# A decoder layer on one core: the order of work in the prologue, and zeros for TensorE before the data comes

## The chip, the core and the metric

The kernel runs on one core of a Trainium2 chip. TensorE multiplies, ScalarE evaluates functions and evacuates results, VectorE and GpSimd do elementwise work, and SyncE issues the transfers from HBM. The engines run side by side, each through its own list of instructions in order; they wait for each other only at semaphores. The metric is the time of one execution on the device in microseconds (us), as the median of several runs.

## The reference

One decoder layer over 4 sequences of 256 tokens with 256 features, in f32, batch-wise independent:

```
x = x + attn(layernorm(x))     # 16 heads: q,k = layernorm(silu(causal conv4(h @ Wq|Wk)));
                               # v = h @ Wv; beta = sigmoid(h @ Wb + bb); gate = silu(h @ Wg)
                               # S_t = (1-b_t) S_(t-1) + b_t v_t k_t^T;  o_t = S_t q_t;  (o*gate) @ Wo
x = x + xattn(layernorm(x))    # query, key = ctx @ Wq.T + bq, ctx @ Wk.T + bk; softmax(query key^T)
x = x + moe(layernorm(x))      # 16 routed experts (4 chosen per token) + a shared one
```

What matters here: the first step of everything is a layer norm of x, while the query and key of the cross attention depend on the context input alone, and are not needed until the 16 heads are done.

## The kernel before

The 1024 tokens are eight tiles of 128, or two halves (`c` = 0, 1) of 512. Weights and activations of the projections are split into a high half, which is a copy rounded to `fp32r`, and a low half, the f32 value minus that copy; `mm3` (L1344 to L1348) makes one product as three: high by low, low by high, high by high. ScalarE makes the high copies of weights (`high`, L605), GpSimd the low halves (`split_low`, L437). Plain f32 products go through `mm` (L1341).

The program has a section for each engine, and in each the instructions are written in the order in which they run; loops are unrolled in pairs of heads. No scheduler changes it. The heads run as a software pipeline in steps. Ahead of that stands a prologue:

- SyncE issues the loads in the order x (two halves), the context's weights, the context, its biases, the identity, beta's weights, and then the weights of the first two heads.
- VectorE clears two tiles (`obetT`, L989, and `dmask`, L990), takes statistics of x (`x_stats`), works out the norm factors (`norm_factors`, signalled by `ln_rstd`), and normalises four of the eight tiles (`half_norm`, L977). ScalarE normalises the other four (L585). Then VectorE copies the identity into parts of `dmask` (L1004, L1005); the columns P to L of each of its four blocks stay zero.
- TensorE makes four context products (`context_qk`, L1362) and 16 transposes of the normalised tiles (`half_transpose`, L1350), three products ahead of the transposes and one behind. ScalarE evacuates the products (`context_out`, L597) and copies the transposed tiles out as `xT_hi` (`half_out`, L589); VectorE makes `xT_lo` (`half_low`, L981).
- `project_in(0, 0, 0)` is the first head's first projection. It needs `w_lo` of the first head and both halves of `xT`. From here on TensorE's list is dense: projections of q, then beta, then k and gate, and so on. ScalarE and VectorE take their results through the taps of the convolution (`first_taps`, L625; `taps`), GpSimd adds the last tap (`last_tap`, L453).
- `wv_hi` and `wv_lo` are the split value weights of the first pair of heads. ScalarE's functions come in tables; where the next function isn't in the loaded one, an `ACT_TABLE_LOAD` stands ahead of it (Sigmoid at L716, Silu at L652).

Of the kernel before, what the change touches and what calls it, by code (L numbers as in the profile page):

```python
# [22 lines left out]
ACT = mybir.ActivationFunctionType  # L23
AX = mybir.AxisListType

P = 128
B, L, D = 4, 256, 256
# [3 lines left out]
N = 512  # L31
# [16 lines left out]
ROUTED_SCALE = 2.5  # L48
EPS = 1e-5
RSQRT_SEED = 1597463007.0  # L50
VERY_NEGATIVE = -3.0e38
# [75 lines left out]
def decoder_layer(nc, x_in, ctx_in, xw_in, xb_in, wb_in, bb_in, w_in, prm_in, wv_in, wo_in,  # L127
# [5 lines left out]
    with ctx:  # L133
# [3 lines left out]
        def sem(name):  # L137
            return ctx.enter_context(nc.semaphore(name))
# [143 lines left out]
        b_lo_ready, r_lo_ready = sem("b_lo_ready"), sem("r_lo_ready")  # L282
        obet_ready, dmask_ready = sem("obet_ready"), sem("dmask_ready")
        r_full, r_score = sem("r_full"), sem("r_score")
        r_tok_full, r_tok_ready = sem("r_tok_full"), sem("r_tok_ready")
# [150 lines left out]
        def _(pool):  # L436
# [36 lines left out]

            pool.wait_ge(ln_rstd, NCH)
            split_low(0, 0)
            low_values(0, 0)
            split_low(0, 1)
            last_tap(0, 0, range(2 * NCH))

# [100 lines left out]
        def _(act):  # L580
# [16 lines left out]
            def context_out(u):  # L597
# [3 lines left out]
                                     bias=xb[:, u // NCH:u // NCH + 1]).then_inc(x_qk_ready, 1)  # L601

            act.wait_ge(ld["beta"], 32)
            nc.scalar.activation(wb_hi, wb, ACT.Copy).then_inc(small_split, 1)
            def high(g, k):  # L605

                s = k % 2
                w = slice(s * 3 * D, (s + 1) * 3 * D)
                act.wait_ge(ld_w[s], uses(g, k, 2) * 16)
                if not (isinstance(g, int) and G * g + k < 2):  # L610

                    act.wait_ge(a_full, units(g, k - 1, 6))
                nc.scalar.activation(w_hi[:, w], w_raw[:, w], ACT.Copy).then_inc(w_hi_ready, 1)
# [80 lines left out]
            def high_projection(pair, s):  # L694
# [3 lines left out]
                nc.scalar.activation(wo_hi[:, w], wo_raw[:, :], ACT.Copy).then_inc(wo_hi_ready, 1)  # L698

            high(0, 0)  # L700
            act.wait_ge(ld_wv[0], 16)
            nc.scalar.activation(wv_hi[:, 0:N], wv_raw[:, 0:N], ACT.Copy).then_inc(wv_hi_ready, 1)
            context_out(0)
            context_out(1)
            for c in range(NCH):
                half_norm(0, c)
            context_out(2)
            for c in range(NCH):
                half_out(0, c, xT_hi)
            context_out(3)  # L710
            high(0, 1)
            first_taps(0, 0, (0, 1))

            for c in range(NCH):
                act.wait_ge(b_full, c + 1)
                nc.scalar.activation(betaT[:, c * N:(c + 1) * N], bank[2 + c][0:H, :], ACT.Sigmoid,  # L716
                                     bias=bb).then_inc(b_ready, 1)
            first_taps(0, 0, (2, 3))
            gates(0, 0, range(NCH))
            first_taps(0, 1, (0, 1))  # L720
# [196 lines left out]
        def _(dve):  # L917
# [70 lines left out]

            obet_zero = steps.did(nc.vector.memset(obetT, 0.0))  # L989
            a = steps.did(nc.vector.memset(dmask[:, :], 0.0))  # L990

# [8 lines left out]
            dve.wait_ge(ld["const"], 16)  # L1000
            steps.after(a)
            dm = dmask[:, :].rearrange("p (b c) -> p b c", b=B)
# [105 lines left out]
            dve.wait_ge(b_ready, NCH)  # L1108
            steps.after(obet_zero)
            bt = betaT.rearrange("h (b t) -> h b t", b=B)  # L1110
# [229 lines left out]
        def _(pe):  # L1340
# [26 lines left out]

            context_qk(0)
            context_qk(1)
            pe.wait_ge(ld["const"], 16)  # L1370
            context_qk(2)
            for c in range(NCH):
                half_transpose(0, c)
            context_qk(3)

# [457 lines left out]
```

## Time and profile before

| | us |
|---|---|
| median of 3 runs | 578.58 (578.08 to 578.64) |
| the profiled execution | 578.73 |
| its span, first to last instruction | 576.9 |
| TensorE busy | 554.7 (96%) |
| VectorE, ScalarE, GpSimd busy | 432.5, 398.1, 292.7 |
| mean granted clock of TensorE | 0.997 |

The span is what the trace shows; the 1.8 us around it are start and end of the execution. A row of the timeline gives the start in us from the first instruction, the length, engine, line, operation and tiles (out<-in), how many instructions are merged in it, and in brackets the idle time of the engine just ahead and what ended it. Tiles that share memory have the name of the memory: `values` is also the normalised x, `raw` the context, `gate` also beta's weights, `gated_hi` also their high half. PE is TensorE, ACT ScalarE, DVE VectorE, POOL GpSimd, SPq SyncE's queue.

### The profile page before, as it was taken

The page shows a single profiled execution, that of the slowest core. Times are in us where ns is not written, and L with a number is a line of the kernel's source. Part 1 is how long each engine was busy: PE and PEld are TensorE (multiplying, and loading weights), DVE is VectorE, ACT ScalarE, POOL GpSimd, SP SyncE. Part 2 cuts the span into 40 slices and gives each one's busy share as a digit, 9 for nine tenths or more (in the row PEclk, how much of TensorE's full clock was granted, in tenths as well). Part 3 has the DMA queues.
Part 4 walks back from the last instruction along what each step waited for, and adds up shares of the span by engine and source line. Part 5 has one row for each costly group of instructions (what it writes and reads, how often), then busy time and mean ns, then how long its engine had stood idle before and what let it go on. Part 6 is the DMA issues. An engine that isn't in the chain of part 4 may idle for free.

```text
span 576.9 us, 9944 instructions
## 1 busy us (share of the span) xinstructions
PE 554.7 (96%) x3392; PEld 485.0 (84%) x3392; DVE 432.5 (75%) x1046; ACT 398.1 (69%) x782; POOL 292.7 (51%) x194
## 2 busy tenths in 40 slices
PE   4898999999999999999999999989899999999997
PEld 1597889989989999899899898878678888888887
DVE  8769989998998899889989998978956543323333
ACT  3979988979779789798797887786653334333431
POOL 2335756746666457366565673420021565556552
PEclk9999999999999999999999999999999999999999
DMA  6132032032030130230211202210020433233321
GB/s 201 31 120 84 0 120 84 1 119 83 3 120 25 59 120 2 82 107 15 84 51 70 83 1 102 82 30 2 1 56 5 164 129 98 95 129 127 94 81 73
DMA packets 18001, 42.31 MB, mean 73 GB/s; under 512 B 4736, under 2 KB 6528, under 8 KB 17952
## 3 DMA queue, kind: packets, MB, share of 16 engines
q1 hardware_dynamic: 17952, 41.69, 21.6%
q8 instruction: 27, 0.44, 0.3%
q14 instruction: 22, 0.18, 0.1%
HBM read 40.47 MB, written 1.21 MB: 72 GB/s over the span
## 4 chain that ended last, share of the span: by engine, by line
PE 85%; DVE 7%; ACT 4%; issue 1%; DMA 1%; SPq 1%; DVEq 0%; ACTq 0%
PE bank L1346 21%; PE bank L1348 20%; PE bank L1347 20%; PE bank L1342 14%; PE bank L1486 5%; PE bank L1474 4%; ACT tok L671 2%; DMA w_raw<-in_w 1%; DVE stats L1051 1%; DVE xT_lo L986 1%; DVE stats L971 1%; DVE x L1187 1%; ACT values L585 1%; DVE x L1336 0%; DVE raw L1070 0%
## 5 line engine op out<-in xcount | busy, mean ns | idle before, releaser
L1346 PE MATMUL bank<-xT_lo,w_hi 128*128 128x512 f32 x320 | 133.7, 418 | 1.9 <-DVE conv L1070 1.2
L1348 PE MATMUL bank<-xT_hi,w_hi 128*128 128x512 f32 x320 | 125.9, 394 | 0.0
L1347 PE MATMUL bank<-xT_hi,w_lo 128*128 128x512 f32 x320 | 125.3, 392 | 0.0
L464 POOL TENSOR_TENSOR gated_lo<-gated,gated_hi 128x512 fp32r<-128x512 f32 x30 | 38.8, 1293 | 116.5 <-ACT gated_hi L691 112.8
L671 ACT ACTIVATE tok<-bank,nmr,rstd 128x128 f32<-128x128 f32 x256 | 91.2, 503 | 2.0 <-DVE nmr L966 2.0
L1346 PEld LDWEIGHTS bank<-xT_lo,w_hi 128*128 128x128 f32 x320 | 60.5, 189 | 16.3 <-DVE conv L1070 3.2
L459 POOL TENSOR_TENSOR raw<-tap,raw 128x506 f32<-128x506 f32 x32 | 62.0, 1936 | 20.3 <-DVE raw L1070 16.3
L459 POOL TENSOR_TENSOR conv<-tap,conv 128x506 f32<-128x506 f32 x32 | 62.0, 1936 | 20.1 <-DVE conv L1070 20.1
L1348 PEld LDWEIGHTS bank<-xT_hi,w_hi 128*128 128x128 f32 x320 | 60.2, 188 | 13.6
L1347 PEld LDWEIGHTS bank<-xT_hi,w_lo 128*128 128x128 f32 x320 | 60.7, 190 | 9.1
L1051 DVE BATCH_NORM_STATS2 stats<-bank 128x6 f32<-128x128 f32 x256 | 56.4, 284 | 14.8 <-PE bank L1474 14.8
L1042 DVE TENSOR_TENSOR_SCAN decay<-obet,dmask 128x1536 f32<-128x1536 f32 x16 | 62.0, 3873 | 0.0
L1226 DVE TENSOR_TENSOR conv<-bank,tok 128x512 f32<-128x512 f32 x36 | 24.8, 690 | 44.2 <-PE bank L1348 44.0
L1234 DVE TENSOR_TENSOR gated_lo<-gate,gated_hi 128x512 fp32r<-128x512 f32 x32 | 24.0, 785 | 39.6 <-ACT gated_hi L849 39.6
L546 POOL TENSOR_TENSOR gate<-conv,tap 128x512 f32<-128x512 f32 x32 | 42.5, 1332 | 21.4 <-DVE conv L1226 13.2
L849 ACT ACTIVATE gated_hi<-gate 128x512 fp32r<-128x512 f32 x32 | 18.9, 628 | 48.0 <-PE bank L1348 41.0
L683 ACT ACTIVATE qk<-bank,prm 128x512 f32<-128x512 f32 x64 | 51.5, 844 | 0.0
L1070 DVE SCALAR_TENSOR_TENSOR raw<-bank,prm,raw 128x510 f32<-128x510 f32 x64 | 46.8, 743 | 5.6 <-ACT tap L639 4.5
L1342 PE MATMUL bank<-qk 128*128 128x256 f32 (+1 forms) x256 | 50.2, 329 | 0.5 <-DVE x L1103 0.3
L1070 DVE SCALAR_TENSOR_TENSOR conv<-bank,prm,conv 128x510 f32<-128x510 f32 x64 | 46.8, 743 | 3.4 <-ACT tap L639 2.3
L1342 PEld LDWEIGHTS bank<-qk 128*128 128x128 f32 x256 | 43.2, 190 | 5.7 <-issue 0.7
L1342 PE MATMUL bank<-probs,values 128*128 128x256 f32 (+1 forms) x256 | 47.0, 327 | 0.0
(184 smaller groups left out, 1398.4 us busy)
## 6 DMA issues: line engine op xcount, KB each, us to landing
obet<-obet_rows SPq DMA_DIRECT2D x16, 768.0 KB, 4.3
w_raw<-in_w SPq DMA_DIRECT2D x22, 384.0 KB, 4.8
tap<-route_rows SPq DMA_DIRECT2D x16, 512.0 KB, 4.0
w_raw<-in_w SPq DMA_DIRECT2D x12, 256.0 KB, 3.0
wv_raw<-in_wv SPq DMA_DIRECT2D x8, 256.0 KB, 4.8
wo_raw<-in_wo SPq DMA_DIRECT2D x8, 256.0 KB, 4.9
w_raw<-in_w SPq DMA_DIRECT2D x12, 128.0 KB, 2.1
x<-in_x SPq DMA_DIRECT2D x2, 512.0 KB, 4.7
```

What stands on the lines that cost most here:

```text
L459: nc.gpsimd.tensor_tensor(y, r, y, ALU.add).then_inc(conv_done, 1)
L464: nc.gpsimd.tensor_tensor(gated_lo[:, cc], gated[:, c * N:(c + 1) * N], gated_hi[:, cc].bitcast(F32), ALU.subtract).then_inc(gated_lo_read ...
L546: nc.gpsimd.tensor_tensor(weighted(m, c), prod[:, two(m, c)], wbc[:, s * T + c * N:s * T + (c + 1) * N], ALU.mult).then_inc(e_weighted, 1)
L671: ins = nc.scalar.activation(tok[:, t * P:(t + 1) * P], t_ring[u][:, i * P:(i + 1) * P], ACT.Identity, scale=rstd[:, t:t + 1], bias=nmr[:, ...
L683: nc.scalar.activation(qk[:, u * N:(u + 1) * N], t_ring[u][:, :], ACT.Identity, scale=prm[:, o:o + 1], bias=prm[:, o + 1:o + 2]).then_inc( ...
L1042: nc.vector.tensor_tensor_scan(decay[:, :], obet[:, :], dmask[:, :], 0.0, ALU.mult, ALU.add).then_inc(decay_ready, 1)
L1051: ins = nc.vector.bn_stats(stats[:, 6 * t:6 * t + 6], t_ring[u][:, i * P:(i + 1) * P])
L1070: ins = nc.vector.scalar_tensor_tensor(out=y, in0=r, scalar=prm[:, o + 3 - back:o + 4 - back], in1=y, op0=ALU.mult, op1=ALU.add)
L1342: return nc.tensor.matmul(o, l, r, start=start, stop=stop)
L1346: nc.tensor.matmul(o, l_hi, r_lo, start=start, stop=False, skip_group_check=loose)
L1347: nc.tensor.matmul(o, l_lo, r_hi, start=False, stop=False, skip_group_check=loose)
L1348: return nc.tensor.matmul(o, l_hi, r_hi, start=False, stop=stop, skip_group_check=loose)
```

## The change

Six things in the prologue; nothing behind it is touched.

1. TensorE multiplies zeros. VectorE clears `dmask` first and signals it by a new semaphore `zeros_ready`. TensorE waits for it, and makes `WARM` = 7 f32 products of 128 zeros by 256 columns of zeros from `dmask` into banks 0 and 1, which nobody reads before the transposes overwrite them.
2. All four context products stand in front of the transposes.
3. ScalarE evaluates a Sigmoid of one column of zeros as its first function.
4. ScalarE's list: layer norm first, then the first head's weights, the transposed activations and two of the context evacuations; the second head's weights go behind beta's Sigmoid, the value weights and the other two evacuations further back, among the gates.
5. GpSimd waits for VectorE's four norm tiles (`ln_norm_dve`) instead of the norm factors, and splits the second head's weights ahead of the first head's last taps; the value weights come between the taps.
6. VectorE's waits for its own clears go through `zeros_ready`.

```
 # GpSimd
-            pool.wait_ge(ln_rstd, NCH)
+            pool.wait_ge(ln_norm_dve, 2 * NCH)
             split_low(0, 0)
+            split_low(0, 1)
+            last_tap(0, 0, (0, 1))
             low_values(0, 0)
-            split_low(0, 1)
-            last_tap(0, 0, range(2 * NCH))
+            last_tap(0, 0, (2, 3))
 # ScalarE
+            act.wait_ge(zeros_ready, 1)
+            nc.scalar.activation(small[:, 0:1], dmask[:, P:P + 1], ACT.Sigmoid)
             act.wait_ge(ld["beta"], 32)
             nc.scalar.activation(wb_hi, wb, ACT.Copy).then_inc(small_split, 1)
...
+            for c in range(NCH):
+                half_norm(0, c)
             high(0, 0)
-            act.wait_ge(ld_wv[0], 16)
-            nc.scalar.activation(wv_hi[:, 0:N], wv_raw[:, 0:N], ACT.Copy).then_inc(wv_hi_ready, 1)
+            for c in range(NCH):
+                half_out(0, c, xT_hi)
             context_out(0)
             context_out(1)
-            for c in range(NCH):
-                half_norm(0, c)
-            context_out(2)
-            for c in range(NCH):
-                half_out(0, c, xT_hi)
-            context_out(3)
-            high(0, 1)
             first_taps(0, 0, (0, 1))
 
             for c in range(NCH):
...
+            high(0, 1)
             first_taps(0, 0, (2, 3))
-            gates(0, 0, range(NCH))
+            act.wait_ge(ld_wv[0], 16)
+            nc.scalar.activation(wv_hi[:, 0:N], wv_raw[:, 0:N], ACT.Copy).then_inc(wv_hi_ready, 1)
+            gates(0, 0, (0,))
+            context_out(2)
+            gates(0, 0, (1,))
+            context_out(3)
             first_taps(0, 1, (0, 1))
 # VectorE
-            obet_zero = steps.did(nc.vector.memset(obetT, 0.0))
-            a = steps.did(nc.vector.memset(dmask[:, :], 0.0))
+            nc.vector.memset(dmask[:, :], 0.0).then_inc(zeros_ready, 1)
+            nc.vector.memset(obetT, 0.0).then_inc(zeros_ready, 1)
...
-            steps.after(a)
+            dve.wait_ge(zeros_ready, 1)
 # TensorE
-            context_qk(0)
-            context_qk(1)
+            pe.wait_ge(zeros_ready, 1)
+            zeros = dmask[:, :].rearrange("p (b c) -> p b c", b=B)
+            for i in range(WARM):
+                mm(bank[i % 2][:, 0:L].rearrange("p (b c) -> p b c", b=2), zeros[:, 0, P:L], zeros[:, 2:4, P:L],
+                   True, True)
+            for u in range(2 * NCH):
+                context_qk(u)
             pe.wait_ge(ld["const"], 16)
-            context_qk(2)
             for c in range(NCH):
                 half_transpose(0, c)
-            context_qk(3)
```

How the lists stand on the two engines in front of the first projection, in the order in which they run. TensorE, from its first product to the first projection (`raw` holds the context, `values` the normalised x), before:

```order
L1342 MATMUL bank<-raw 128x512 [waits ld_ctx] x2
L1342 MATMUL bank<-raw 128x512 [waits ld_ctx,ld_const]
L1357 MATMUL bank<-ident,values 128x128 [waits ln_norm_dve,ln_norm_act]
L1357 MATMUL bank<-ident,values 128x128 x7
L1357 MATMUL bank<-ident,values 128x128 [waits ln_norm_dve,ln_norm_act]
L1357 MATMUL bank<-ident,values 128x128 x7
L1342 MATMUL bank<-raw 128x512 [waits ld_ctx]
L1346 MATMUL bank<-xT_lo,w_hi 128x512 [waits w_lo_ready,ln_split]
```

and now:

```order
L1350 MATMUL bank<-dmask 128x256 [waits zeros_ready]
L1350 MATMUL bank<-dmask 128x256 x6
L1350 MATMUL bank<-raw 128x512 [waits ld_ctx] x4
L1365 MATMUL bank<-ident,values 128x128 [waits ln_norm_dve,ln_norm_act,ld_const]
L1365 MATMUL bank<-ident,values 128x128 x7
L1365 MATMUL bank<-ident,values 128x128 [waits ln_norm_dve,ln_norm_act]
L1365 MATMUL bank<-ident,values 128x128 x7
L1354 MATMUL bank<-xT_lo,w_hi 128x512 [waits w_lo_ready,ln_split]
```

Seven products from `dmask` stand in front, the fourth context product has gone ahead of the transposes, and the first projection waits for the same two things as before.

ScalarE, from its first data to the taps of the first head (`attT<-bank` is a context evacuation, `values<-x` a norm tile, `xT_hi<-bank` a copy of transposed activations), before:

```order
L604 ACTIVATE gated_hi<-gate 128x32 [waits ld_beta]
L613 ACTIVATE w_hi<-w_raw 128x768 [waits ld_w0]
L702 ACTIVATE wv_hi<-wv_raw 128x512 [waits ld_wv0]
L600 ACTIVATE attT<-bank,xbias 128x512 [waits x_qk_full] x2
L585 ACTIVATE values<-x,nmr,rstd 128x256 [waits ln_rstd]
L585 ACTIVATE values<-x,nmr,rstd 128x256
L585 ACTIVATE values<-x,nmr,rstd 128x256 [waits ln_rstd]
L585 ACTIVATE values<-x,nmr,rstd 128x256
L600 ACTIVATE attT<-bank,xbias 128x512 [waits x_qk_full]
L593 ACTIVATE xT_hi<-bank 128x512 [waits ln_full] x4
L600 ACTIVATE attT<-bank,xbias 128x512 [waits x_qk_full]
L613 ACTIVATE w_hi<-w_raw 128x768 [waits ld_w1]
```

and now:

```order
L608 ACTIVATE small<-dmask 128x1 [waits zeros_ready]
L610 ACTIVATE gated_hi<-gate 128x32 [waits ld_beta]
L588 ACTIVATE values<-x,nmr,rstd 128x256 [waits ln_rstd]
L588 ACTIVATE values<-x,nmr,rstd 128x256
L588 ACTIVATE values<-x,nmr,rstd 128x256 [waits ln_rstd]
L588 ACTIVATE values<-x,nmr,rstd 128x256
L620 ACTIVATE w_hi<-w_raw 128x768 [waits ld_w0]
L596 ACTIVATE xT_hi<-bank 128x512 [waits ln_full] x4
L603 ACTIVATE attT<-bank,xbias 128x512 [waits x_qk_full] x2
L644 ACTIVATE conv<-bank,prm 128x512 [waits a_full,ld_prm0]
L646 ACTIVATE tap<-bank,prm 128x512
```

The norm tiles and the four copies have moved past the value weights and all context evacuations; two of the evacuations stand right behind the copies. The value weights, the other evacuations and the second head's weights are no longer in this stretch.

GpSimd, from its first split to the first head's last taps (`conv<-tap`), before:

```order
L444 TENSOR_TENSOR w_lo<-w_raw,w_hi 128x768 [waits w_hi_ready,ln_rstd]
L450 TENSOR_TENSOR wv_lo<-wv_raw,wv_hi 128x512 [waits wv_hi_ready]
L444 TENSOR_TENSOR w_lo<-w_raw,w_hi 128x768 [waits w_hi_ready]
L459 TENSOR_TENSOR conv<-tap,conv 128x2x253 [waits taps_done] x4
L459 TENSOR_TENSOR raw<-tap,raw 128x2x253 [waits taps_done]
```

and now:

```order
L446 TENSOR_TENSOR w_lo<-w_raw,w_hi 128x768 [waits w_hi_ready,ln_norm_dve]
L446 TENSOR_TENSOR w_lo<-w_raw,w_hi 128x768 [waits w_hi_ready]
L461 TENSOR_TENSOR conv<-tap,conv 128x2x253 [waits taps_done] x2
L452 TENSOR_TENSOR wv_lo<-wv_raw,wv_hi 128x512 [waits wv_hi_ready]
L461 TENSOR_TENSOR conv<-tap,conv 128x2x253 [waits taps_done] x2
L461 TENSOR_TENSOR raw<-tap,raw 128x2x253 [waits taps_done]
```

The first split waits for `ln_norm_dve`, and the second head's split has moved past the value split, which now stands between two pairs of taps.

## Rows read from the trace of the kernel before

**Rows 1.** The page, part 1: busy us, share, instructions.

```profile
PE 554.7 (96%) x3392; PEld 485.0 (84%) x3392; DVE 432.5 (75%) x1046; ACT 398.1 (69%) x782; POOL 292.7 (51%) x194
```

**Rows 2.** Chain of waits, 9 to 20 us and 47: start, length, what.

```profile
4.83 5.33 DMA w_raw<-in_w
...
10.18 0.84 ACT w_hi L613
11.03 0.52 ACT wv_hi L702
11.55 1.25 ACT attT L600 x2
12.80 1.97 ACT values L585 x4
14.76 0.57 ACT attT L600
15.34 0.49 ACT xT_hi L593
...
15.85 1.30 DVE xT_lo L986 x2
...
17.19 0.50 PE bank L1346
...
47.28 0.23 PE bank L1347
```

**Rows 3.** Timeline, TensorE: start, length, what, count.

```profile
8.29 5.38 PE L1342 MATMUL bank<-raw 128*128 128x512 f32 x6 [8.29 <-DMA xbias<-in_xb]
...
12.72 0.95 PE L1342 MATMUL bank<-raw 128*128 128x512 f32 x1
...
13.83 2.08 PE L1357 MATMUL bank<-ident,values 128*128 128x128 f32 x16 [0.16 <-ACT values L585]
15.74 1.02 PE L1342 MATMUL bank<-raw 128*128 128x512 f32 x2
...
16.18 0.59 PE L1342 MATMUL bank<-raw 128*128 128x512 f32 x1
...
30.41 0.40 PE L1346 MATMUL bank<-xT_lo,w_hi 128*128 128x512 f32 x1
```

**Rows 4.** Timeline, VectorE.

```profile
1.11 1.34 DVE L989 MEMSET gate<- 16x1536 f32 x1 [1.11 <-PEq L1825]
...
10.16 0.17 DVE L966 SCALAR_TENSOR_TENSOR nmr<-nw,rstd 128x8 f32<-128x8 f32 x1
...
11.34 1.90 DVE L977 TENSOR_SCALAR values<-x,rstd,nmr 128x256 f32<-128x256 f32 x1
...
13.16 1.30 DVE L1004 COPY dmask<-ident 128x128 f32<-128x128 f32 x1
...
33.53 2.97 DVE L1070 SCALAR_TENSOR_TENSOR raw<-bank,prm,raw 128x510 f32<-128x510 f32 x4 [4.47 <-ACT tap L639]
```

**Rows 5.** Timeline, GpSimd.

```profile
11.17 1.92 POOL L444 TENSOR_TENSOR w_lo<-w_raw,w_hi 128x768 fp32r<-128x768 f32 x1 [10.73 <-ACT w_hi L613]
13.05 1.33 POOL L450 TENSOR_TENSOR wv_lo<-wv_raw,wv_hi 128x512 fp32r<-128x512 f32 x1
...
35.14 1.28 POOL L459 TENSOR_TENSOR raw<-tap,raw 128x506 f32<-128x506 f32 x1 [4.93 <-DVE raw L1070]
```

**Rows 6.** Timeline, ScalarE.

```profile
21.64 1.28 ACT L716 ACT_TABLE_LOAD   x1
...
24.43 0.78 ACT L637 ACTIVATE conv<-bank,prm 128x512 f32<-128x512 f32 x1 [0.24 <-PE bank L1348]
...
34.61 2.19 ACT L659 ACTIVATE conv<-conv 128x512 f32<-128x512 f32 x4
```

**Rows 7.** Windows: PE, PEld, DVE, ACT, POOL busy, PEclk, DMA.

```profile
43.00:47.00 4.00, 1.77 (x14) 1.33 (x13) 3.89 (x8) 3.57 (x11) 2.74 (x3) 1.00 0.01 2
8.00:13.80 5.80, 5.38 (x6) 1.83 (x6) 5.38 (x19) 3.85 (x8) 2.63 (x2) 1.00 0.44 163
```

More of the change, by code:

```diff
@@ L49 @@
 EPS = 1e-5
+WARM = 7
 RSQRT_SEED = 1597463007.0
@@ L283, in decoder_layer @@
         obet_ready, dmask_ready = sem("obet_ready"), sem("dmask_ready")
+        zeros_ready = sem("zeros_ready")
         r_full, r_score = sem("r_full"), sem("r_score")
@@ L1108, in _ @@
             dve.wait_ge(b_ready, NCH)
-            steps.after(obet_zero)
+            dve.wait_ge(zeros_ready, 2)
             bt = betaT.rearrange("h (b t) -> h b t", b=B)
```

## The prediction

> **What bounds the kernel now.** I read the page first: TensorE is busy 554.7 us, 96% of the span [rows 1]. Nothing that the change touches lies behind the first head, so the question is how early TensorE's dense stream begins and whether everything behind it moves along. The second view is the chain of waits up to that beginning [rows 2]. It runs from the load of the first head's weights (lands at 10.16) through ScalarE alone: the split copy of those weights at 10.18 (0.84 us), the split of the value weights at 11.03 (0.52), two evacuations of context products at 11.55 (1.25), four layer norm tiles at 12.80 (1.97), a third evacuation at 14.76 (0.57), the first copy of the transposed activations at 15.34 (0.49). Then VectorE makes two low halves from 15.85 (1.30), and the first projection product starts at 17.19. The reader is to see that ScalarE is busy without a gap for 5.2 us there, and that 0.52 + 1.25 + 0.57 = 2.34 us of it are not needed by the product at 17.19.
>
> Third, TensorE's own timeline [rows 3]: it starts at 8.29, when the context has landed, with six passes of 512 columns (three of the four context products; an f32 product is two passes). The last starts at 12.72, so they come 0.89 us apart; the two passes of the fourth product, at 15.74 and 16.18, are 0.44 apart. The first six therefore ran at the 1.2 GHz level and the later two at 2.4 GHz, although the granted clock of the stretch 8.00 to 13.80 is given as 1.00 [rows 7]: here the pace tells the level, not the column. The 16 transposes from 13.83, in 2.08 us, are fast already. So the clock rose between 12.72 and 13.83, after 4.4 to 5.5 us of these passes.
>
> Fourth, VectorE and GpSimd [rows 4, 5]. The norm factors end at 10.16 + 0.17 = 10.33. Three of VectorE's four norm tiles fit between that and 11.34, 0.34 us each; the fourth takes 1.90 us from there, and the first copy into dmask 1.30 from 13.16, while GpSimd splits weights from 11.17 (1.92) and 13.05 (1.33): both end when a GpSimd instruction does.
>
> **The change part by part.**
>
> Zeros on TensorE. The first memset runs from 1.11 for 1.34 us [rows 4]; dmask's is now that one, so the zeros can start at about 2.5. Seven products of 256 columns are 14 passes of 0.89 / 2 = 0.44 us at the low level, 6.2 us: they end at 8.7 if the clock never rises meanwhile, and earlier if it does. 4.4 to 5.5 us after 2.5 is 6.9 to 8.0, so I take the clock as high when the context products start at about 8.5 (0.2 later than now, on their load). Four products are then 8 passes of 0.44, 3.5 us, to 12.0, with the fourth, which stood behind the transposes, in front.
>
> Norms first on ScalarE. They start at 10.37 instead of 12.80 and end at 10.37 + 1.97 = 12.34. VectorE's tiles, which GpSimd no longer disturbs since it now waits for them, end at about 11.34 + 0.34 = 11.7. The transposes start at about 12.0 (0.13 us each, 2.08 / 16), those of the second half at about 13.0, and the first bank, four of them, is full by 12.6. The weights' split copy follows the norms: 12.34 to 13.18. The copies of the transposed activations start there, at 13.2 instead of 15.34. From that copy to the product the chain takes 17.19 - 15.34 = 1.85 us: **15.05**. In other words the chain loses 2.34 us of other work and gains 0.19 in waiting for the norm factors (10.37 against 10.18), which is -2.15.
>
> GpSimd behind the norms. This puts a second operand on the path. The weights' high half is ready at 13.18 instead of 11.02, so the low half runs from 13.25 for 1.92 us [rows 5] and ends at 15.17: **15.2** with the step to TensorE. Before, it was done at 13.09 and hidden. It is now late by about the same as VectorE's half, and I take the later one: the first product starts at 15.2, **2.0 us earlier**. What is late next is GpSimd's split, then VectorE's.
>
> What that split collides with. The dmask copies lay between 13.16 and VectorE's next work at 15.85, blocked until GpSimd's end at 14.38; so their own time is at most 15.85 - 14.38 = 1.47 us, and from 11.7 they are over at 13.2, before it starts. VectorE's low halves run from 13.7 beside it. The nearest rows are GpSimd's add at 35.14, 1.28 us, beside VectorE's taps from 33.53, four in 2.97 us or 0.74 each [rows 4, 5]: VectorE reads PSUM there as in the low halves, and neither side stretches. I cost it at nothing; if they did exclude each other, VectorE would wait until 15.15, and the product would start 1.85 - 0.49 = 1.36 later, at 16.5. The Trainium skill, "SBUF — State Buffer", section "Who interferes with whom", says the same of the mechanism: the shared port pair is an exclusive lock, which VectorE's copies and scalar forms and its operations with two SBUF inputs take, and one with a single SBUF input doesn't. By that rule the two stretched rows at 11.34 and 13.16 are explained (the trace agrees, 1.90 against 0.34), and the low halves, with one input in PSUM, go free.
>
> Sigmoid's table first. Its load of 1.28 us at 21.64 [rows 6] goes; the first load, before any data has come, merely loads another table. It is worth nothing here: after it the next taps wait 0.24 us for TensorE at 24.43, so ScalarE had slack. Into that slack goes the split of the second head's weights (0.84), which stood ahead of the first taps. The second sigmoid waits for 24 products (12 of the projection, 12 of beta) at 0.23 [rows 2]: 15.2 + 5.5 + 0.4 = 21.1; with its own 0.6 and the split ScalarE is free at 22.5, against 24.43 - 2.0 = 22.4. GpSimd's split for the second head follows and ends at 24.4; TensorE needs it at 30.41 - 2.0 = 28.4 [rows 3]. GpSimd's value split now queues behind, with two taps ahead of it and two after it, until 24.4 + 4 x 1.28 + 1.33 = 30.9; ScalarE's Silu of the first head needs them at 34.61 - 2.0 = 32.6 [rows 6]. The value split copy and two context evacuations (0.52 + 2 x 0.6 us) fall into ScalarE's waits for TensorE ahead of 32; if they didn't, the second head's taps would be late by up to 0.5. On the queue the load of the third head's weights, which waits for the first split, leaves 2 us later than at present, and belongs to a head whose products come after 28.4; the loads behind it wait for beta, which comes earlier.
>
> Sum, against the profiled execution's 578.73 (span 576.9 and 1.8 around it; the median of the runs is 0.15 lower): -2.0 at the first product, 0 at every later step because each later wait of the prologue is on TensorE or on something that TensorE released. 578.6 - 2.0 = **576.6**. Ends: -2.15 if only ScalarE's chain counted, -1.4 if three passes of the context products were still slow (0.44 us more each, of which 0.6 is free, since the first bank is needed only at 13.2, and 0.15 by GpSimd's being later). The runs of before spread over 0.56 us, which is added to these.
>
> **The rivals.**
>
> *The zeros do not raise the clock.* Multiplying zeros may not be what raises it, or the moment may lie later than 4.4 to 5.5 us; no run here multiplies zeros. Then the context products start cold at 8.7; with the clock up 5.5 us later, at 14.2, six passes are slow, the transposes start at 15.0, the first bank is full at 15.5, and the product comes at 17.35: 578.7, no change. Against it: the six slow passes show that f32 passes do raise it. The trace has one rise, and cannot show the spread.
>
> *GpSimd and VectorE exclude each other after all.* Product at 16.5, gain 0.7: 577.9. The taps beside GpSimd's add speak against it [rows 4, 5].
>
> *A later step takes part of it back*, ScalarE's fuller list between 16 and 30 us or GpSimd's longer queue: each would show as a TensorE wait of 0.3 to 1 us: 577.2 to 577.9.
>
> *Slower: the clock falls before the first product.* The fourth context product no longer stands behind the transposes, so TensorE idles from about 13.9 to 15.2. If the clock went down there, the products would start at the 1.2 GHz level and stay on it for 4.4 to 5.5 us, as at the start; in that time half the work gets done, which costs 2.2 to 2.75 us, more than the 2.0 gained: 578.8 to 579.4. It decides once the first projection products come 0.46 apart instead of 0.23. Against it: between 43 and 47 us TensorE is busy 1.77 of 4.00 us, and the products right behind come 0.23 apart [rows 2, 7].
>
> **How the numbers follow.** Forecast 0.74 (its own range 576.0 to 577.1), no rise 0.09, exclusion 0.05, a later step 0.07, slower 0.05. The range 575.9 to 577.9 takes in the forecast, the exclusion and most of the later steps, and leaves out the no-change and the slower case. About 0.2%, 1.16 us, is what a measurement of this kernel can tell from no change, so faster means below 577.4: the forecast, half of the later steps and a share of the early ends of the other cases, 0.82; same 0.13; slower 0.05.
>
> **What would show it.** Right: zeros from about 2.5; context passes 0.44 apart, from 8.3 to 8.7 on; ScalarE's norms at 10.4; VectorE's fourth norm tile as short as its first; first product at 15.0 to 15.4, released by GpSimd's w_lo or VectorE's xT_lo; the gap to before still 1.8 to 2.1 us at 30 and at 50 us. Wrong: context passes 0.89 apart, or the first product at 16.4 or later, or a new TensorE wait before 50 us that brings the stream back to before's times.

## The result, and the profile after

The changed kernel takes 575.03 us (median of 9 runs, 574.92 to 576.86); the kernel before, run beside it, 578.53 (9 runs, 578.08 to 578.64). The ratio of the changed kernel's time to that of before is 0.9949, with a 95% interval of 0.9938 to 0.996 (further down in brackets): 3.5 us faster, where 2.0 was predicted, and below the predicted range. The profiled execution took 574.93 us, with a span of 573.1.

One thing about the numbers has to be said first. The times of either kernel don't scatter, they fall into groups whose medians lie 1.6 us apart. A run has none, one or two stretches of about 3.4 us in which the granted clock is 0.50, the 1.2 GHz level, and the mean granted clock of the run tells which: 0.999 or 1.000 with none, 0.996 or 0.997 with one, 0.993 or 0.994 with two. The fourteen traces show this for none and for one (a fall behind TensorE's last product is not counted); for the other runs the number of stretches is read from the mean clock, and no run with two was traced. In all runs of this study, counting the repeats of both kernels beside the experiments (the first nine runs of before are placed by their times):

| | no stretch: runs, median | one: runs, median | two |
|---|---|---|---|
| before | 25 of 86, 576.95 | 60 of 86, 578.50 | 1, 580.11 |
| changed | 12 of 30, 574.97 | 16 of 30, 576.56 | 2, 578.03 and 578.16 |
| difference | −1.98 | −1.94 | |

The prologue's rows first, in the order of the rows of before. The page, part 1 (busy us, share of the span, instructions), beside [rows 1]:

```profile
PE 554.8 (97%) x3406; PEld 487.2 (85%) x3406; DVE 428.9 (75%) x1046; ACT 396.9 (69%) x782; POOL 292.9 (51%) x194
```

TensorE's busy time is as before, with 14 instructions more, the zeros. The chain of waits (start, length, what), beside [rows 2]:

```profile
1.17 5.26 DMA x<-in_x
...
6.46 1.42 DVE stats L979 x4
...
10.39 2.07 ACT values L588 x4
12.46 0.75 ACT w_hi L620
...
13.35 1.82 POOL w_lo L446
...
15.31 0.47 PE bank L1354
```

The load of x, VectorE's statistics, ScalarE's four norm tiles, the weights' split copy, GpSimd's low half, the product. The value weights and the three context evacuations are gone from it, and the chain starts from x where it had started from w. TensorE (start, length, instruction, count, in brackets the idle time ahead and what ended it), beside [rows 3]:

```profile
2.52 4.89 PE L1350 MATMUL bank<-dmask 128*128 128x256 f32 x14 [2.52 <-DVE dmask L997]
8.33 3.70 PE L1350 MATMUL bank<-raw 128*128 128x512 f32 x8 [0.93 <-DMA xbias<-in_xb]
11.87 1.91 PE L1365 MATMUL bank<-ident,values 128*128 128x128 f32 x16
15.31 0.47 PE L1354 MATMUL bank<-xT_lo,w_hi 128*128 128x512 f32 x1 [1.53 <-POOL w_lo L446]
...
25.54 0.50 PE L1354 MATMUL bank<-xT_lo,w_hi 128*128 128x512 f32 x1 [1.19 <-DVE conv L1078]
...
28.47 0.39 PE L1354 MATMUL bank<-xT_lo,w_hi 128*128 128x512 f32 x1
```

The eight context passes take 3.70 us, 0.46 each, where the first six had taken 0.89. The first product comes at 15.31 instead of 17.19 and is released by GpSimd; the second head's product comes at 28.47 instead of 30.41. The timelines of the other three engines follow. VectorE of the changed kernel, beside [rows 4]:

```profile
10.39 1.38 DVE L985 TENSOR_SCALAR values<-x,rstd,nmr 128x256 f32<-128x256 f32 x4
...
13.71 2.48 DVE L994 TENSOR_TENSOR xT_lo<-bank,xT_hi 128x512 fp32r<-128x512 f32 x4 [0.85 <-ACT xT_hi L596]
```

GpSimd of the changed kernel, beside [rows 5]:

```profile
13.35 1.81 POOL L446 TENSOR_TENSOR w_lo<-w_raw,w_hi 128x768 fp32r<-128x768 f32 x1 [12.91 <-ACT w_hi L620]
22.57 1.93 POOL L446 TENSOR_TENSOR w_lo<-w_raw,w_hi 128x768 fp32r<-128x768 f32 x1 [7.41 <-ACT w_hi L620]
```

ScalarE of the changed kernel, beside [rows 6]:

```profile
10.39 2.07 ACT L588 ACTIVATE values<-x,nmr,rstd 128x256 f32<-128x256 f32 x4 [1.33 <-DVE nmr L974]
...
13.10 2.02 ACT L596 ACTIVATE xT_hi<-bank 128x512 fp32r<-128x512 f32 x4
...
22.50 0.78 ACT L644 ACTIVATE conv<-bank,prm 128x512 f32<-128x512 f32 x1
```

VectorE's four norm tiles take 1.38 us together; the one that ran beside GpSimd before had taken 1.90 alone. VectorE's four low halves take 2.48 us beside GpSimd's split, as they did before with GpSimd idle:

```profile
15.85 2.48 DVE L986 TENSOR_TENSOR xT_lo<-bank,xT_hi 128x512 fp32r<-128x512 f32 x4 [0.43 <-ACT xT_hi L593]
```

GpSimd's 1.81 is no longer than its 1.92 before: the two did not exclude each other.

So far this is about the predicted 2.0 us: these two traces lie 1.88 us apart at the first product, 1.94 at the second head's, and still 1.97 at four transposes some 15 us later (43.02 against 44.99). Most of the rest lies 400 us later, where the change does nothing. Here are the windows of before (start and end, length, busy time and count of each engine; the last three columns are the granted clock, DMA's share and GB/s):

```profile
414.00:415.50 1.50, 0.03 (x1) 0.00 (x0) 1.17 (x2) 1.50 (x4) 0.00 (x0) 1.00 0.00 0
...
416.50:419.50 3.00, 3.00 (x8) 1.93 (x7) 2.62 (x17) 0.98 (x1) 0.00 (x0) 0.50 0.00 0
```

TensorE's timeline of before in these windows:

```profile
415.67 0.41 PE L1346 MATMUL bank<-xT_lo,wv_hi 128*16 128x512 f32 x1 [1.65 <-DVE xT_lo L986]
...
416.54 0.63 PE L1346 MATMUL bank<-xT_lo,wv_hi 128*16 128x512 f32 x1
416.97 0.63 PE L1347 MATMUL bank<-xT_hi,wv_lo 128*16 128x512 f32 x1
```

The windows of the same place in the changed kernel:

```profile
411.84:413.34 1.50, 0.03 (x1) 0.00 (x0) 1.17 (x2) 1.50 (x4) 0.00 (x0) 1.00 0.00 0
...
414.00:417.50 3.50, 3.50 (x17) 2.58 (x16) 3.09 (x18) 2.15 (x4) 0.00 (x0) 1.00 0.00 0
```

TensorE's timeline of the changed kernel there:

```profile
413.51 0.40 PE L1354 MATMUL bank<-xT_lo,wv_hi 128*16 128x512 f32 x1 [1.64 <-DVE xT_lo L994]
...
414.22 0.40 PE L1354 MATMUL bank<-xT_lo,wv_hi 128*16 128x512 f32 x1
414.45 0.39 PE L1355 MATMUL bank<-xT_hi,wv_lo 128*16 128x512 f32 x1
```

The stall is the same (1.65 and 1.64 us, for VectorE's low half of the second group of tokens). Behind it the products of before come 0.43 us apart at a granted clock of 0.50, until about 419.6; those of the changed kernel come 0.23 apart at 1.00. The changed kernel is 2.16 us ahead where the stall ends (413.51 against 415.67) and 3.8 at the end of the span (573.1 against 576.9): the stretch is the 1.6 us between, and no instruction there differs.

### The profile page after: what moved, and what is told of

It reads as the page before. It is cut to its first block, busy times and chain, and to the rows that moved or that the text cites. A ratio compares the mean times of both kernels' runs of the same rounds, so it can differ in the third digit from the quotient of the medians.

```text
span 573.1 us, 9971 instructions
## 1 busy us (share of the span) xinstructions
PE 554.8 (97%) x3406; PEld 487.2 (85%) x3406; DVE 428.9 (75%) x1046; ACT 396.9 (69%) x782; POOL 292.9 (51%) x194
## 4 chain that ended last, share of the span: by engine, by line
PE 85%; DVE 8%; ACT 4%; issue 1%; DMA 1%; POOL 0%; SPq 0%; DVEq 0%; ACTq 0%; POOLq 0%
PE bank L1354 21%; PE bank L1356 20%; PE bank L1355 20%; PE bank L1350 14%; PE bank L1498 5%; PE bank L1486 4%; ACT tok L678 2%; DMA x<-in_x 1%; DVE stats L979 1%; DVE stats L1059 1%; ACT values L588 1%; DVE x L1195 1%; DVE x L1344 0%; DVE raw L1078 0%; DVE xT_lo L994 0%
```

## The experiments

The first theory (S in the quoted expectations) was that the 3.5 us are two things: 2.0 in the prologue, as predicted, and 1.6 from the stretch at 416, which the profiled run of before has and that of the changed kernel has not; its rival (D), that the lists of ScalarE and GpSimd later in the prologue give the rest. When the first experiments had shown groups of times, two theories stood against each other: M, that each run has a stretch behind a TensorE stall or none, and that the kernel sets how often; and C, that the share of such runs belongs to the chip or the hour and is the same for both kernels. In experiments 9 and 10, A and B are two answers on one term of the prediction.

**1. The new order without zeros.** The changed kernel with

```diff
-WARM = 7
+WARM = 0
```

> The changed kernel without its seven products of zeros. Both theories: the context passes run at the 1.2 GHz level again, six of them 0.89 us apart from 8.3, so the transposes start at about 14.5 instead of 11.9 and the first projection product comes at 16.9 to 17.1 (changed 15.31, before 17.19). Theory S, that the rest of the gain is the slow stretch of TensorE at 416 us in the kernel before, which comes or stays away with the same stall of TensorE ahead of it: 578.2 to 578.4 where it comes, 576.5 to 576.7 where it doesn't; if the time at which the stall comes decides it, most runs stay at 578.3. Rival D, that the rest of the gain comes from the new order of ScalarE's and GpSimd's lists later in the prologue: about 577.0 in all runs.

Measured: 577.11 (12 runs), ratio 0.999 [0.9979, 1.0001]; without a stretch 576.93 (7 runs), as before; with one 577.66 (5 runs, 577.53 to 577.97), 0.8 below before's. Neither theory had named the times with one. TensorE's timeline:

```profile
8.48 6.06 PE L1350 MATMUL bank<-raw 128*128 128x512 f32 x8 [8.48 <-DMA xbias<-in_xb]
14.37 1.91 PE L1365 MATMUL bank<-ident,values 128*128 128x128 f32 x16
16.98 0.50 PE L1354 MATMUL bank<-xT_lo,w_hi 128*128 128x512 f32 x1 [0.70 <-DVE xT_lo L994]
```

The eight context passes take 6.06 us instead of 3.70, hold up the transposes until 14.37, and the product comes 0.2 us earlier than before. The traced run is one of three at 576.43 to 576.54; the other four without a stretch are at 576.93 to 577.18. Without a risen clock the order is worth nothing in these four and 0.4 to 0.5 us in the three. Where the other five runs have their stretch, and why it costs them less, was not traced.

**2. The zeros without the order.** On the kernel before, with `WARM` = 7 (VectorE's two later waits for its clears go through `zeros_ready` too):

```diff
-            obet_zero = steps.did(nc.vector.memset(obetT, 0.0))
-            a = steps.did(nc.vector.memset(dmask[:, :], 0.0))
+            nc.vector.memset(dmask[:, :], 0.0).then_inc(zeros_ready, 1)
+            nc.vector.memset(obetT, 0.0).then_inc(zeros_ready, 1)
...
+            pe.wait_ge(zeros_ready, 1)
+            zeros = dmask[:, :].rearrange("p (b c) -> p b c", b=B)
+            for i in range(WARM):
+                mm(bank[i % 2][:, 0:L].rearrange("p (b c) -> p b c", b=2), zeros[:, 0, P:L], zeros[:, 2:4, P:L],
+                   True, True)
             context_qk(0)
```

> The kernel before with the seven products of zeros in front (and dmask cleared first), every other list as before. Both theories: the first projection product stays at 17.1 to 17.2, since ScalarE's list sets it. Theory S: if the moment at which TensorE's early work raises the clock decides the slow stretch at 416 us, 576.8 in most runs; if the time of the stall decides it, 578.5. Rival D: 578.5 in all runs.

Measured: 577.50 (11 runs), ratio 0.999 [0.9979, 1.0]; without a stretch 576.34 and 576.38, 0.6 below before's median, from two runs only; the other 9 of 11 runs have a stretch, with a median of 577.54, 1.0 below before's. Windows of the profiled run, and then TensorE's timeline of it:

```profile
11.20:13.50 2.30, 0.00 (x1) 0.00 (x0) 2.30 (x2) 2.30 (x6) 2.30 (x2) 1.00 0.00 0
...
15.00:18.00 3.00, 3.00 (x10) 1.81 (x9) 2.81 (x8) 2.15 (x6) 0.00 (x0) 0.50 0.12 39
```

```profile
2.52 6.05 PE L1344 MATMUL bank<-dmask 128*128 128x256 f32 x14 [2.52 <-DVE dmask L991]
8.40 2.80 PE L1344 MATMUL bank<-raw 128*128 128x512 f32 x6
13.51 2.55 PE L1359 MATMUL bank<-ident,values 128*128 128x128 f32 x16 [2.31 <-ACT values L587]
...
16.87 1.32 PE L1348 MATMUL bank<-xT_lo,w_hi 128*128 128x512 f32 x1
```

The context passes end early, TensorE stands for 2.31 us until ScalarE's norms, and some 1.4 us after it has begun again the clock goes to 0.50; the first product takes 1.32 us. This is what the prediction's slower rival feared, the lower level at the first product, though the stall is another: ahead of the transposes and not behind them. This run is 1.1 us longer than the two without. The product comes earlier than the expected 17.1 to 17.2, but not for the zeros alone: here the weights landed at 9.95 (10.16 in the trace of before), and in experiment 3's trace, whose prologue is that of before and whose weights also land at 9.95, the product comes at 16.89. How the zeros gain the 0.6 us is not shown.

**3, 4. Filling the stall at 414.** Three products of zeros into a free bank, on the kernel before and on the changed one:

```diff
             half_transpose(2, 0)
+            z = dmask[:, :].rearrange("p (b c) -> p b c", b=B)
+            for i in range(FILL):      # 3
+                mm(bank[2][:, 0:L].rearrange("p (b c) -> p b c", b=2), z[:, 0, P:L], z[:, 2:4, P:L], True, True)
```

> The kernel before with three products of zeros (f32, 256 columns, 1.3 us at full clock) on TensorE in the stall of 1.65 us at 414 us, ahead of the router's products. Theory S: the clock does not fall at 416, the products there come 0.23 apart, and the time is 576.8 (578.5 less 3.4 us at half rate, 1.7) in all runs. Rival D: 578.5, or a little more if the zeros delay the router.

> The changed kernel with the same three products of zeros in the stall. Theory S: every run at 574.9 to 575.1, none near 576.5. Rival D: the two groups of times of the changed kernel remain, two thirds at 575.0 and one third at 576.4 to 576.9.

Measured: before with the fill 578.27 (12 runs), ratio 0.9996 [0.9985, 1.0008]: none 5 runs (576.99), one 6, two 1. The changed kernel with it 575.04 (6 runs), ratio 0.9949 [0.9936, 0.9962]: none 5, one 1. The first theory's 576.8 in every run failed. The windows of the first one's profiled run, about another stall, that of 1.19 us ahead of 27.19 (TensorE waits for VectorE's taps):

```profile
26.00:27.10 1.10, 0.00 (x0) 0.00 (x0) 1.06 (x3) 1.08 (x3) 0.00 (x0) 1.00 0.66 89
...
28.50:31.50 3.00, 3.00 (x8) 2.26 (x7) 0.27 (x2) 0.60 (x1) 1.26 (x1) 0.50 0.85 272
```

This run had no stretch at 416, and one at 28.3. So it isn't one place: several stalls can have one behind them.

**5, 11. The changed kernel, unedited, again.**

> The changed kernel once more, for the shares of its two groups of times. Theory M (mixture): a run has one stretch of 3.4 us at the 1.2 GHz level behind a TensorE stall, or none; the group without it moved from 576.9 to 575.0 (the prologue, -1.95), the group with it from 578.5 to 576.6, and the share of runs with it fell from 27 of 38 to 4 of 15. Two groups again, 575.0 and 576.4 to 576.9, the upper one with a quarter to a half of the runs. Rival C, that the two groups belong to the chip or the hour and not to the kernel: the share of the upper group is that of the kernel before in this same call.

> The changed kernel a third time, to count. Theory M: 575.0 at clock 0.999 to 1.0, 576.4 to 576.9 at 0.996 to 0.997, 578.1 at 0.994; of the 21 runs so far 9, 10 and 2. If the change itself made the slow stretch rarer than in the kernel before (18 of 61 without), well over half of these runs come at 575.0; if the first nine runs of it were luck, about 4 in 10.

Measured: 576.51 (12 runs), ratio 0.9976 [0.9963, 0.999], with 3 runs without a stretch, 7 with one, 2 with two; and 576.53 (9 runs), ratio 0.9961 [0.9948, 0.9974], with 3, 6 and none. The same program is at 575.0 in one session and at 576.5 in the next two. In these two, the share of runs with a stretch (9 of 12, then 6 of 9) is that of before beside it (16 of 23, then 18 of 25), as theory C had it. The first repeat's profiled run has its stretch at a third place, in its windows and then in TensorE's timeline:

```profile
41.00:45.00 4.00, 1.78 (x14) 1.34 (x13) 3.88 (x8) 3.56 (x11) 2.73 (x3) 1.00 0.01 2
45.00:45.50 0.50, 0.50 (x4) 0.41 (x3) 0.50 (x2) 0.50 (x3) 0.50 (x1) 0.90 0.00 0
45.50:48.50 3.00, 3.00 (x11) 2.43 (x10) 3.00 (x1) 3.00 (x8) 3.00 (x2) 0.50 0.00 0
```

```profile
43.00 0.66 PE L1498 MATMUL bank<-ident,tok 128*128 128x128 f32 x4 [1.48 <-ACT tok L678]
44.40 0.66 PE L1498 MATMUL bank<-ident,tok 128*128 128x128 f32 x4 [0.74 <-ACT tok L678]
...
45.73 0.63 PE L1354 MATMUL bank<-xT_lo,w_hi 128*128 128x512 f32 x1
```

TensorE stalls for 1.48 and 0.74 us, with four transposes between; the granted clock is 1.00 until 45, 0.90 on average over the next half microsecond, and 0.50 from there.

**6, 7. Filling more stalls.** The kernel before with the fill at 414 and two products of zeros behind beta's transposes, in the stall ahead of 27; the changed kernel with the same two, and with two of the four context products put behind the transposes again, in the stall ahead of the first projection:

```diff
             beta_tokens()
+            fill(3, FILL_EARLY)        # 2
...
             half_transpose(2, 0)
+            fill(2, FILL)              # 3
```

```diff
-            for u in range(2 * NCH):
+            for u in range(HEAD_CTX):  # 2
                 context_qk(u)
...
+            for u in range(HEAD_CTX, 2 * NCH):
+                context_qk(u)
```

> The kernel before with zeros on TensorE in two of its stalls: two products behind beta's transposes (stall of 1.2 us at 26 us) and three behind the transposes at 414 us. Theory M: nearly all runs at 576.9 to 577.0, the upper group at 578.5 gone or below 2 in 10. Rival C: half or more of the runs still at 578.5. If the fills were only in the way: all runs later by up to 0.3.

> The changed kernel with the same two fills, and with the third and fourth context products behind the transposes, where TensorE stalls 1.5 us ahead of the first projection product. Theory M: all runs at 575.0, none at 576.4 or above. Rival C: the two groups of the changed kernel, at the share of the call.

Measured: 577.59 (12 runs), ratio 0.9996 [0.9985, 1.0008], 6 without and 6 with one, where theory M had expected fewer than 2 in 10 with one; its profiled run has it at 46.0 to 49.4, behind the stall that no zeros fill. And 574.99 (6 runs), ratio 0.9958 [0.9943, 0.9973], 5 without and 1 with one, which theory M had not expected at all. The fills cost nothing (576.89 and 574.95 without a stretch).

**8, 12. The weights' split first.** A version that the profile pointed to: ScalarE stands idle until 10.39 in the changed kernel, and the weights land at about 10, so their split copy can go ahead of the norms, and GpSimd's split comes off the end of the path. As experiment 7, with three context products in front and

```diff
+            high(0, 0)
             for c in range(NCH):
                 half_norm(0, c)
-            high(0, 0)
```

and VectorE's copies into dmask behind its low halves.

> As the one before, but with the first head's weights split on ScalarE ahead of its norm tiles (they land at 10.2, the norm factors come at 10.4), the dmask copies on VectorE behind its low halves, and only the fourth context product behind the transposes. GpSimd's split then runs from 11.8 to 13.6 and no longer ends last; ScalarE's first copy of the transposed activations starts at 12.95 instead of 13.10, and the first projection product comes 1.9 later, at 14.85 (changed 15.31): 574.5 to 574.6 in all runs. If GpSimd's split was not what ended last in the changed kernel, 575.0.

> The weights-first version with both fills and the fourth context product behind the transposes, a second time: 574.2 to 574.5 at clock 0.999 to 1.0, 575.7 to 576.1 at 0.996; the upper group in about 1 of 6 if the fills keep the clock up at three of its four stalls, in half or more if the single run of it in six was luck.

Measured: 574.37 (6 runs), ratio 0.9948 [0.9932, 0.9964], and 574.48 (6 runs), ratio 0.9943 [0.9925, 0.9961]; 9 of 12 runs without a stretch, median 574.36 (574.5 to 574.6 in all runs was expected). GpSimd's timeline of the first, and then TensorE's:

```profile
11.81 1.83 POOL L448 TENSOR_TENSOR w_lo<-w_raw,w_hi 128x768 fp32r<-128x768 f32 x1 [11.37 <-DVE values L987]
```

```profile
14.58 0.50 PE L1356 MATMUL bank<-xT_lo,w_hi 128*128 128x512 f32 x1
```

GpSimd is done at 13.64, and the product comes at 14.58, 0.7 us earlier than in the changed kernel and 0.3 earlier than expected; the end comes 0.6 earlier. In its chain the product now follows the transposes and the fourth context product on TensorE itself. The fills cost and gain nothing without a stretch (experiment 7), so the 0.6 us belongs to the weights' split and the moved copies together. This version beats both kernels: by 2.6 us where before has no stretch either (574.36 against 576.95), and by about 4 us of before's median.

**9. Without Sigmoid's table first.** The changed kernel less

```diff
-            act.wait_ge(zeros_ready, 1)
-            nc.scalar.activation(small[:, 0:1], dmask[:, P:P + 1], ACT.Sigmoid)
```

> The changed kernel without the Sigmoid of zeros in front, so that Sigmoid's table is loaded (1.28 us) between the first taps and beta's first Sigmoid again, at about 19.7. The prediction costed that at nothing. Theory A, nothing: runs at clock 0.999 to 1.0 stay at 575.0. Theory B, that in the new order ScalarE has no slack left there: its second Sigmoid, which started at 21.08 after 0.69 us of waiting, ends 0.5 to 0.6 later, the second head's weights and the taps of k behind it too, and these runs come at 575.5 to 575.6.

Measured: 576.97 (12 runs), ratio 0.9986 [0.997, 1.0001]; without a stretch 575.31 and 575.38, against 574.97, and with one 576.94 (6 runs), against 576.56; the other four runs have two (578.34 to 578.50). The table is worth 0.4. ScalarE's timeline, and then TensorE's:

```profile
19.76 1.28 ACT L716 ACT_TABLE_LOAD   x1
...
22.94 0.76 ACT L642 ACTIVATE conv<-bank,prm 128x512 f32<-128x512 f32 x1
```

```profile
25.95 0.50 PE L1352 MATMUL bank<-xT_lo,w_hi 128*128 128x512 f32 x1 [1.55 <-DVE conv L1076]
```

The load stands ahead of the Sigmoids again, the taps start at 22.94 instead of 22.50, and TensorE waits 1.55 us for them instead of 1.19.

**10. GpSimd's list as before.** The changed kernel with

```diff
-            pool.wait_ge(ln_norm_dve, 2 * NCH)
+            pool.wait_ge(ln_rstd, NCH)
             split_low(0, 0)
-            split_low(0, 1)
-            last_tap(0, 0, (0, 1))
             low_values(0, 0)
-            last_tap(0, 0, (2, 3))
+            split_low(0, 1)
+            last_tap(0, 0, range(2 * NCH))
```

> The changed kernel with GpSimd's list as before (first split on the norm factors, value split, second head's split, four taps). Theory A: the first split starts at 13.3 as in the changed kernel, since the weights' high half comes at 13.2 anyway; but the value split waits for its high half at 25.7, the second head's split ends at 28.9 instead of 24.5, and the second head's first product, at 28.47 in the changed kernel, is 0.5 late: runs at clock 0.999 to 1.0 at 575.4 to 575.5. Theory B: the order on GpSimd is worth nothing, 575.0.

Measured: 576.97 (11 runs), ratio 0.997 [0.9958, 0.9983]; without a stretch 575.53 (4 runs), with one 577.06 (6 runs): the order is worth 0.5 to 0.55. GpSimd's timeline, and then TensorE's:

```profile
27.07 1.84 POOL L446 TENSOR_TENSOR w_lo<-w_raw,w_hi 128x768 fp32r<-128x768 f32 x1
```

```profile
15.35 0.47 PE L1353 MATMUL bank<-xT_lo,w_hi 128*128 128x512 f32 x1 [1.55 <-POOL w_lo L446]
...
28.96 0.50 PE L1353 MATMUL bank<-xT_lo,w_hi 128*128 128x512 f32 x1 [0.26 <-POOL w_lo L446]
```

The first split, and with it the first product, stand where they did (15.35). The value weights' split copy is late on ScalarE now, and the second head's split, queued behind it on GpSimd, ends at 28.91 where it had run from 22.57: TensorE waits 0.26 us for it, and the product comes 0.49 us later than the changed kernel's at 28.47.

## Why the prediction was wrong

**The prologue: right, within 0.1 us.** Zeros from 2.52, context passes at 0.46, norms at 10.39, copies at 13.10, GpSimd's split from 13.35 to 15.17 as the last, product at 15.31 (predicted 15.2; 15.29 to 15.35 in the traces of experiments 4, 5, 9, 10 and 11, which leave this stretch as it is). The difference at equal clock is 1.98 us without a stretch and 1.94 with one, against 2.0. That one trace of before was enough is in part luck: by experiment 3's trace the same prologue can bring the product 0.3 us earlier, at 16.89. That GpSimd's wait makes its split the new end of the path was right too: experiment 8 takes it off and gains 0.6. The zeros and the order need each other: by the medians without a stretch, the order alone gives 0.0 us (0.5 at best), the zeros alone 0.6 (two runs), both 2.0. That the clock would be high when the context products start was right in all ten traces with zeros, but once only just. In experiment 9's trace all 14 passes of zeros run at the lower level's pace (14 of 0.44 us are 6.2), and only the context passes are fast:

```profile
2.52 6.13 PE L1348 MATMUL bank<-dmask 128*128 128x256 f32 x14 [2.52 <-DVE dmask L995]
8.48 3.70 PE L1348 MATMUL bank<-raw 128*128 128x512 f32 x8
```

**The step that failed is the sum's frame: "578.6 - 2.0", with "0 at every later step".** The base held a stretch of 1.6 us, and I took its time for the kernel's own. All nine runs of before in the first session had one, by their times (578.08 to 578.64); of the changed kernel's nine, six had none. So the median compared 578.53 with 575.03: 1.58 of stretch (578.53 − 576.95) and 1.98 of prologue are 3.56, and 3.50 was measured. In the next sessions the changed kernel's median, 576.5, is where the forecast had put it, with before at 578.4 and 578.5: there both medians hold a stretch, and a time that came out right would have been luck. The view that showed it was at hand: the profiled run's mean clock, 0.997, stood in the table, and I read the granted clock only from 8 to 13.8 and from 43 to 47 us, not at 416.5 to 419.5. The range failed for the same reason: it was made of the prologue's terms and before's spread of 0.56 us, and all of those runs were of one group.

**Whether the change itself makes stretches rarer stays open.** 12 of 30 runs without one, against 25 of 86, is no clear difference, and 0 of 9 against 6 of 9 in one session was what made it look like one.

**The argument against the slower rival was unsound.** I held that the clock does not fall in a short stall because one trace had kept it up behind the gaps at 43 to 47 us [rows 7]. Experiments 5, 6, 9, 10 and 11 have their stretch at that very place, in other runs of nearly the same instructions, and experiment 2 has it ahead of the first product. The fall is real, by the run; at the first product it cost 1.1 us in experiment 2's trace, and 1.1 to 1.8 in all eight traces that have one, and not the 2.2 to 2.75 that I took from the rise at the start: the lower level lasted about 3.4 us, not 4.4 to 5.5. In the changed kernel's profiled run the stall of 1.53 us before 15.31 left the clock up. The Trainium skill, "TensorE: Matmul & The Clock Gate", Part 1, which the prediction weighed, says that the moment of the rise shifts from run to run; the trace agrees, in that the same 14 passes of zeros took 4.89 us in one and 6.13 in another. Whether a like shift decides if a fall comes at all is not shown by any run.

**Two terms costed at nothing were not nothing.** "It is worth nothing here" for Sigmoid's table: 0.4 us (experiment 9). I had read the slack from a wait of 0.24 us at 24.43 [rows 6], less than the load's 1.28, and had put the second head's split into the same slack; by the prediction's own sum ScalarE was then free at 22.5 where 22.4 was needed, so nothing was left for the load. GpSimd's order got no term at all, only the check that its consumers would not wait: 0.5 to 0.55 us (experiment 10). Both are inside the measured 2.0: without either, a later step takes that much of the earlier start back.

**Exclusion of GpSimd and VectorE:** rightly costed at nothing (GpSimd's 1.81 us beside VectorE's 2.48, which took 2.48 alone as well).

## What to carry to other kernels

Before a time is taken as a base, look at the granted clock over the whole span and at the mean clock of every run: a stretch at the lower level is a cost that no edit of the instructions shows, and a median over runs with and without it moves by its whole price. Compare runs with equal clock, and take one trace's clock behind a stall for one throw, not for a rule. Where the end of a path is moved to another engine, ask next what stands ahead of it there: the split that ended last here could be put first.

## What the runs showed of the hardware that was not expected

- In eight of the fourteen traces a TensorE stall of 1.2 to 2.3 us (or two, of 1.48 and 0.74) next to transposes is followed by about 3.4 us at a granted clock of 0.50, beginning some 0.5 to 1.5 us after the engine has resumed (in experiment 6, after the first of the two stalls). Other runs of the same program have none: 25 of 86 runs of before. The products in such a stretch come 0.43 us apart instead of 0.23, and the traced runs are 1.1 to 1.8 us longer than runs of the same kernel without one.
- That the stall brings the stretch is likely and not proven. In the profiled runs no filled stall had a stretch behind it, which single runs cannot prove. Over the four filled versions of the changed kernel (experiments 4, 7, 8, 12) 19 of 24 runs had no stretch, against 12 of 30 unfilled; on the kernel before it was 11 of 24 against 25 of 86, which is not clear. Why the fill at 414 alone seems to help the changed kernel so much (5 of 6 runs) was not found, since both traced runs of that kernel with a stretch have it at 45 us. The stall at 43 to 45 us was filled in no experiment.
- The rise at the start shifts as well: in ten traces the 14 passes of zeros took 4.89 us (the changed kernel) to 6.13 (experiment 9), where 14 at the lower level would be 6.2.
